# A graph network layer: the subtraction of h moved to TensorE, one normalised row of four moved to VectorE, three more edge groups read from the h table

## The reference

```
h    = relu(layernorm(x))
em   = relu(layernorm([h[src], h[dst]] @ msg_w + msg_b) * g + be) * edge_weight
msgs = segment_sum(em, dst) / count(dst)          # 0 where a node has no edge
gate = sigmoid(h @ gate_w + gate_b)
u    = relu(layernorm([h, msgs] @ upd_w + upd_b) * g_u + be_u)
out  = x + gate * u + (1 - gate) * h
```

## Time and profile before

| | us |
|---|---|
| median of 3 runs (1055.12 to 1071.27) | 1056.28 |
| profiled execution | 1053.59 |
| its span, first to last instruction | 1052.1 |
| busy in the span: PE / DVE / ACT / POOL | 729.7 / 833.7 / 811.5 / 605.7 |
| node stage, roughly | 0 to 560 |
| of it the steady loop, with clock 0.83 | 100 to 540 |
| edge stage, roughly | 560 to 1052 |

### The profile page before, as it was taken

How to read it: one execution, slowest core, us unless ns; L and a number is a source line. 1 busy time by engine, 2 the same in 40 slices (tenths; PEclk the granted TensorE clock), 3 DMA queues, 4 the chain that set the end, 5 groups by cost and what they waited for, 6 DMA issues and landing times.

```text
span 1052.1 us, 20637 instructions
## 1 busy us (share of the span) xinstructions
PE 729.7 (69%) x4448; PEld 588.4 (56%) x4448; DVE 833.7 (79%) x3740; ACT 811.5 (77%) x3396; POOL 605.7 (58%) x602
## 2 busy tenths in 40 slices
PE   2377686776767677777666547777777778778772
PEld 2256565654545556555545336666665667667661
DVE  7287888886877888778789347999999988888984
ACT  2378787877868788778779258999999977878973
POOL 5555555554545555555555746666666666665557
PEclk9787978887888887788776668999989888988986
DMA  5255655565655666566532211322221121111110
GB/s 147 76 177 175 209 182 190 187 200 179 196 173 192 215 198 199 171 200 206 192 117 68 90 38 62 95 92 83 94 89 54 62 70 54 61 63 58 65 67 34
DMA packets 74548, 133.66 MB, mean 127 GB/s; under 512 B 16134, under 2 KB 18006, under 8 KB 74482
## 3 DMA queue, kind: packets, MB, share of 16 engines
q1 hardware_dynamic: 53868, 97.58, 27.1%
q0 software_dynamic: 18912, 34.84, 11.8%
q10 hardware_dynamic: 1702, 0.53, 0.2%
HBM read 56.01 MB, written 80.81 MB: 130 GB/s over the span
## 4 chain that ended last, share of the span: by engine, by line
ACT 47%; PE 16%; another core or an unknown queue 15%; issue 11%; DVE 7%; POOL 3%; ACTq 1%; DMA 0%; DVEq 0%; POOLq 0%; SPq 0%
ACT hrow L406 14%; ACT junk L413 13%; ACT xload L406 4%; ACT work L444 3%; PE py L1290 3%; POOL out L626 3%; PE pt L1248 3%; ACT lnv L388 2%; PE pm L1313 2%; ACT work L1159 2%; PE pm L1315 2%; ACT rs L393 2%; ACT at L1099 1%; PE py L1254 1%
## 5 line engine op out<-in xcount | busy, mean ns | idle before, releaser
L626 POOL DMA_INDIRECT out<-work,sidx x196 | 202.7, 1034 | 135.3 <-issue 54.2
L413 ACT ACTIVATE junk<-py 128x128 bf16<-128x128 f32 x588 | 155.7, 292 | 74.8 <-remote 64.2
L621 POOL DMA_INDIRECT ring<-in_x,gidx x140 | 141.9, 1013 | 89.7 <-DVE work L465 47.4
L406 ACT ACTIVATE hrow<-xload,nb,rs 128x128 f32<-128x128 f32 x392 | 163.9, 525 | 1.6 <-issue 0.8
L621 POOL DMA_INDIRECT ring<-in_x,src_i x116 | 116.3, 1002 | 68.4 <-issue 31.5
L1290 PE MATMUL py<-w_u,work 128*128 128x129 f32 x784 | 144.9, 341 | 0.0
L1290 PEld LDWEIGHTS py<-w_u,work 128*128 128x128 f32 x784 | 122.7, 238 | 28.2 <-issue 28.2
L413 ACT ACTIVATION_READ_ACCUMULATOR junk<-py 128x1 f32 x588 | 130.7, 223 | 0.0
L1254 PE MATMUL py<-bias,ones 3*128 3x258 bf16 x294 | 66.8, 313 | 77.6 <-ACT work L1099 56.8
L621 POOL DMA_INDIRECT work<-in_x,gidx x56 | 55.8, 996 | 108.9 <-DVE work L465 97.9
L1248 PE MATMUL pm<-ident,work 128*128 128x128 f32 x376 | 72.4, 325 | 63.4 <-ACT work L1104 31.9
(11 more groups left out here) (179 smaller groups left out, 2049.0 us busy)
## 6 DMA issues: line engine op xcount, KB each, us to landing
xload<-in_x SPq DMA_DIRECT2D x98, 256.0 KB
normalised_rows<-hrow SPq DMA_DIRECT2D x98, 256.0 KB
out<-work SPq DMA_DIRECT2D x98, 256.0 KB
running_sums<-acc SPq DMA_DIRECT2D x49, 256.0 KB
staged_target_rows<-work SPq DMA_DIRECT2D x14, 256.0 KB
ring<-staged_target_rows SPq DMA_DIRECT2D x14, 256.0 KB, 2.8
out<-work,sidx POOLq DMA_INDIRECT x196
ring<-in_x,gidx POOLq DMA_INDIRECT x140
```

Of the source, the lines that this page charges most:

```text
L406: last = nc.scalar.activation(dest[:, m, :], rows[:, m, :], ACT.Relu, bias=nb[:, s4, at + m:at + m + 1], scale=rs[:, s4, at + m:at + m + 1])
L413: last = nc.scalar.activation(junk[:, j, k, :], prod[:, k, 0:H], ACT.Square, scale=scale, accum_out=mv[:, slot, at + k, 1:2])
L621: pool.indirect_dma_start(out=dest, out_offset=None, in_=rows, in_offset=bass.IndirectOffsetOnAxis(ap=idx, axis=0), **({} if rows is sums_ ...
L626: pool.indirect_dma_start(out=out, out_offset=bass.IndirectOffsetOnAxis(ap=idx, axis=0), in_=rows, in_offset=None, **if_tail).then_inc(s, 16)
```

## The change

- `turned(g)` groups (94 of 98): VectorE's four `mix` operations become one of 128x512, o = max(hrow, 0) + x. omg is no longer computed for them.
- TensorE's `back` becomes four transposes of the rectified rows and, into the same bank, four products of `ht_dst` (h transposed) with `minus_ident`, so that pm = u - h and L776 gives o = gt * (u - h) + (x + h), as before.
- One of the four h rows (LIFTED = 3) leaves ScalarE: VectorE makes it in `lifted_row`, as (x - mean) * rstd without the relu, right after `minus_mean`. So that row goes unrectified into `hrow`, into the h table and through the transposes; the relu is now in the moves out of PSUM (L1099, L1157: Copy becomes Relu) and in the max of the mix.
- New waits: SP's store of `hrow`, TensorE's `flip` wait for `lifted` as well; VectorE's `lifted_row` waits for the store of the group four before; ScalarE's move into `ht_dst` waits for `back` of the group four before, which now reads that buffer.
- One operation in the preparation makes `minus_ident`.
- LATE 29 becomes 26 and UPFRONT 10 becomes 13: edge groups 26 to 28 take their source rows from the h table, and 52 gathers instead of 40 stand between its completion and the first scatter.

```diff
 EARLY = 5
-LATE = 29
-UPFRONT = 10
+LATE = 26
+UPFRONT = 13
+LIFTED = G - 1
 REFILLED = 36
...
             "nb": 1,
-            "gain": 3,
+            "gain": 2,
+            "rest": 1,
             "mix": 1,
...
         }
-        nd = stages("node", {**common, "turned": 1, "back": 1})
+        nd = stages("node", {**common, "turned": 1, "back": 1, "lifted": 1})
         tl = stages("tail", common)
...
                              "gate": 2,
-                             "rest": 1,
                              "msgw": 1,
...
                 L.mark(nc.vector.reciprocal(gt[:, b, 0:n], e1[:, b, 0:n]))
-            else:
-                L.wait()
-                L.mark(nc.vector.tensor_scalar(omg[:, b, 0:n], gt[:, b, 0:n], -1.0, 1.0, ALU.mult, ALU.add))
+
+        def rest(dve, d, g, n=G):
+
+            d["gain"].after(dve, g)
+            b = g.at % 4
+            one_mark(d["rest"], dve, shifted(d, g), nc.vector.tensor_scalar(omg[:, b, 0:n], gt[:, b, 0:n], -1.0, 1.0, ALU.mult,
+                                                                            ALU.add))
...
                     nd["h"].after(sp, q)
+                    nd["lifted"].after(sp, q)
                     if q.turn is None and q.at == NG - 1:
...
                     row_stats(L, s, xload[:, s.at % XS, 1:2], 1)
-                if fin:
-                    gain(dve, nd, g, 2)
                 if new:
...
                     L.mark(row_stats(L, s, xload[:, s.at % XS, 2:4], 2))
+                if fin and not turned(g):
+                    rest(dve, nd, g)
                 if between is not None:
...
                     minus_mean(dve, nd, s.back(1), G)
+                if live(s.back(1), NG):
+                    lifted_row(s.back(1))
                 if new:
...
                     aggregate(L, s, G)
-                if fin:
-                    nd["gain"].after(dve, g)
+                if fin and turned(g):
+                    one_mark(nd["mix"], dve, g, nc.vector.scalar_tensor_tensor(
+                        o[:, g.at % 4], hrow[:, g.at % 4], 0.0, xload[:, g.at % XS], ALU.max, ALU.add))
+                elif fin:
+                    nc.vector.tensor_scalar(o[:, g.at % 4, LIFTED, :], hrow[:, g.at % 4, LIFTED, :], 0.0, None, ALU.max
+                                            ).then_inc(s_raised, 1)
+                    nd["rest"].after(dve, shifted(nd, g))
+                    dve.wait_ge(s_raised, g.at - TURNED + 1)
                     for k in range(G):
-                        last = mix_row(g, k, hrow[:, g.at % 4], xload[:, g.at % XS], o[:, g.at % 4])
+                        h = o if k == LIFTED else hrow
+                        last = mix_row(g, k, h[:, g.at % 4], xload[:, g.at % XS], o[:, g.at % 4])
                     one_mark(nd["mix"], dve, g, last)
-                    if not turned(g):
-                        beta(dve, nd, g, t_buf[:, g.at % 4], be_upd)
+                    beta(dve, nd, g, t_buf[:, g.at % 4], be_upd)
+
+            def lifted_row(g):
+
+                s4 = (g.at + 1) % 4
+                nd["rstd"].after(dve, g.back(-1))
+                if beyond(g, 4):
+                    dve.wait_ge(s_hst[g.at % 4], g.rounds(16))
+                one_mark(nd["lifted"], dve, g, nc.vector.tensor_scalar(
+                    hrow[:, g.at % 4, LIFTED, :], xload[:, g.at % XS, LIFTED, :], mv[:, s4, LIFTED, 0:1],
+                    rs[:, s4, LIFTED:LIFTED + 1], ALU.subtract, ALU.mult))
...
             assert prep_n[0] == BORDERS1, prep_n
+            dve.wait_ge(s_const, 2)
+            nc.vector.tensor_scalar(minus_ident[:, :], ident[:, :], -1.0, None, ALU.mult)
...
                 if live(g, NG):
-                    evacuate(nd, g, ht_dst[:, g.at % 4, :], pt[:, g.at % 2, :], ACT.Copy, "ht", "flip")
+                    node_ht(g)
                 node_h(s)
+
+            def node_ht(g):
+                if beyond(g, 4) and turned(g.back(4)):
+                    nd["back"].after(act, g.back(4))
+                evacuate(nd, g, ht_dst[:, g.at % 4, :], pt[:, g.at % 2, :], ACT.Relu, "ht", "flip")
...
                         act.wait_ge(s_hst[g.at % 4], g.rounds(16))
-                    one_mark(nd["h"], act, g, h_rows(g, hrow[:, g.at % 4], xload[:, g.at % XS], 0))
+                    one_mark(nd["h"], act, g, h_rows(g, hrow[:, g.at % 4], xload[:, g.at % XS, 0:LIFTED], 0))
...
                             act.wait_ge(s_staged[b], 16 * STAGED // 2)
-                    nc.scalar.activation(ht_src[:, g.at % 2, :], pt[:, 0, :], ACT.Copy)
+                    nc.scalar.activation(ht_src[:, g.at % 2, :], pt[:, 0, :], ACT.Relu)
                     ed["flip"].after(act, g)
...
                     if live(n, NG):
-                        evacuate(nd, n, ht_dst[:, n.at % 4, :], pt[:, n.at % 2, :], ACT.Copy, "ht", "flip")
+                        node_ht(n)
                     if turned(node.back(5)):
...
                         nd["final"].after(pe, g.back(1))
-                    one_mark(nd["back"], pe, g, flip(pm[:, :, :].rearrange("p k h -> p (k h)"), t_buf[:, g.at % 4]))
+                    for k in range(G):
+                        nc.tensor.matmul(pm[:, k, :], t_buf[:, g.at % 4, k, :], ident[:, :], start=k == 0, stop=False,
+                                         is_transpose=True)
+                    for k in range(G):
+                        last = nc.tensor.matmul(pm[:, k, :], ht_dst[:, g.at % 4, k * H:(k + 1) * H], minus_ident[:, :],
+                                                start=False, stop=k == G - 1)
+                    one_mark(nd["back"], pe, g, last)
                 g = s.back(4)
...
                     nd["h"].after(pe, g)
+                    nd["lifted"].after(pe, g)
                     one_mark(nd["flip"], pe, g, flip(pt[:, g.at % 2, :], hrow[:, g.at % 4]))
...
             def edge_step(s):
```

6 lines of the change are left out of this document (4 added, 2 removed).

## The result

The changed kernel takes 1090.56 us (median of 4 runs, 1084.9 to 1091.53) beside 1055.7 for the kernel before (1056.28 ahead of its fourth run): 1.0332 times its time, 95% interval 1.0279 to 1.0385. Forecast was 1022; the kernel is slower, as in the rival of 1100 us. The profiled execution of after took 1091.53 us, its span is 1090.4: 38.3 us more than before.

What follows compares the result with a forecast made beforehand. Node loop bound by VectorE and ScalarE at full clock (about 4.1 us), TensorE at half clock (5.1), plus TensorE stalls. Profiled 1053.6 - 34 (node loop) - 1 + 2 (edge stage) = 1020.6, forecast 1022 beside 1056.3; range 965 to 1105.

Steps and rivals of the forecast that it cites:

- the rival of 1100 us: Whole kernel slower, chance 0.28: stalls persist despite more PE work, half clock costs more; 5.75 us a step, 1100 us.
- the choice of the pattern of stalls: Node loop: stalls and half clock between the early and late edge stage's patterns, 4.9 us a step, -34 us.
- the sign I had given: Node loop, 100 to 540 us: if the forecast holds, clock 0.88 or more and unnamed share under 10%.
- My cycle sum: Node loop: a cycle's unstalled time divided by 4.1 us (full clock) and 7.0 (half) gives steps; 4.66, 5.2 or 6.45 each.
- its sign, a clock below 0.8: Node loop: clock below 0.8, with L1104 and L413 waiting for PE every step, would mean the slower case, chance 0.28.
- The good step: Node loop at full clock: PE becomes the bound at 3.7 to 4.58 us, taken as 4.1, no worse than 4.08.
- Half clock: Node loop at half clock: PE's extra products lengthen the step from 5.12 to 7.0 us, which nothing hides.
- Costs of nothing for the lifted row's waits: Node loop: VectorE's and ScalarE's waits for an earlier store of `hrow`, issued 2 to 3 steps ahead, cost nothing.
- The 12 gathers: Edge stage's start: 12 more gathers take 15.6 us, POOL idles 12.8, 2.8 show; +2 us, bounds 0 to 6.
- four steps later: Edge stage's start: the first scatter's successor needs it only four steps later, so the gathers' cost was put at +2 us.
- The sign that I had named: Near 640 us: a gap of POOL's scatters or VectorE waiting for `s_scat` would mean the gathers cost more than +2 us.
- this rival's price of nothing: Node loop: VectorE's lifted row could delay POOL's descriptor writing, at most 0.28 us a step, priced at nothing; no chance given.

Runs made afterwards that it cites:

- g2: Changed kernel without its four products with `minus_ident`, on an occasion with stalls: 1084.87 us, ratio 1.0166 to the kernel before.
- g1: Kernel before with only the changed kernel's TensorE products added, on an occasion with stalls: 1083.01 us, ratio 1.0175 to the kernel before.
- e2: Kernel before with only LATE 26 and UPFRONT 13 changed, on a quiet occasion: 871.78 us, ratio 1.0111 to the kernel before.
- e5: Changed kernel run again unaltered, on a quiet occasion: 846.28 us, ratio 0.9832 to the kernel before.
- e8: Changed kernel plus unread TensorE products ahead of `back`, 18, 8, 8 and 0 in four steps running: 1143.6 us, ratio 1.0710 to the kernel before.
- f1: Kernel before plus four unread TensorE products in every node step: 1067.69 us, ratio 1.0308 to the kernel before.

## Why the prediction was wrong

**The step that failed is the choice of the pattern of stalls**, "I choose between the first and second, 4.9". I read the low unnamed share of the edge stage as a property of PE's mix of work and took it over to the node loop. The clock did what I said (0.89, the sign I had given was 0.88 or more), but the unnamed share went to 21.7%, not below 10%, and the step to 5.55 us, not 4.9. Clock and stalls are separate things: a clock of 0.81 goes with 22.3% in g2, one of 0.89 with 15.7% in g1 and with 21.7% in after. The rule of the Trainium skill that the prediction cites (TensorE: Matmul & The Clock Gate, section HAM oscillation), which the trace bears out as far as the clock goes, would have misled in the same direction. My cycle sum comes near with the right sizes: the eight long pieces from 112.45 to 256.88 us are 20.6 us apart, 4.2 of it stalled, 22% (4.5 us) at half clock; 11.9 / 3.8 + 4.5 / 6.5 = 3.8 steps, 5.4 us each; measured 5.55. It should have been tried on the kernel before first: 7 / 4.1 + 6.8 / 5.12 = 3.0 steps in 17.3 us, 5.7 us each, where 5.28 was measured.

The slower rival was nearly right in its price, 1100 and 5.75 us a step with part of it absorbed, and in its premise that stalls have a cause which more PE work doesn't remove. The rest was partly luck. It kept the stalls as they were and put the whole loss on PE at half clock, while the runs show both more named time with the products (g1) and more stall time with the shorter work (g2); and its sign, a clock below 0.8, didn't come.

The last line of the sum is off by little: 1020.6 and 2.7 give 1023.3, not 1022.

**Full and half clock.** The good step was given 4.1 (3.7 to 4.58) and is 3.77 to 3.85: the sets of transposes queue up back to back, as in my lower bound. Half clock: 7.0 against 6.5. VectorE's new operation 0.67 and 0.66, the lifted row 0.28 and 0.35, so that VectorE's work is 3.99 a step with stalls (316.01 x 5.554 / 440), not 3.87. ScalarE 3.74 and 3.83. On a quiet occasion this part gives 80 x (4.06 - 3.77) = 23 us.

**Waits.** Costs of nothing for the lifted row's waits held: 1.5 us of idle time in 68 (L792 above).

**The 12 gathers** were given +2, bounds 0 to 6. The trace has 13 us between the first and the seventh store with stalls, and e2 has 10.1 us on the whole without. The error is the 12.8 us of POOL idle time that I netted against them: that time is waiting for h rows which themselves come later when the run of gathers is longer, so 10.2 us of it were still there after; and "four steps later" was no cover, since those steps pass in less time than the run takes. The sign that I had named, VectorE waiting for the scatter, is e5's L1014.

**The lifted row and POOL.** The prediction weighed, by the Trainium skill, SBUF, section Who interferes with whom, that VectorE could hold off POOL's descriptor writing. The gathers take 0.998 to 0.999 us each in the node loop of after and 0.996 to 0.997 before: no sign of it. So this rival's price of nothing stands. The bond that the rows do show runs between POOL's gathers and TensorE's results, and the prediction didn't weigh it.

**What stays open:** what the stalls are, and why one occasion has them and another doesn't. Of the 19 above 3 us in after, 18 end within some 2 us of a fall of the clock; they all but vanish where PE is saturated (e8, 1.7% of the chain); and they end behind unbroken runs of POOL's gathers. None of this is shown as the cause.

## What to carry to other kernels

Take the time of the kernel before on more than one occasion ahead of any working: here it is 861 or 1036 to 1072 us, and the same edit is 1.7% faster on the one and 3.3% slower on the other. Where the chain holds a large unnamed share, price an edit for both cases, with and without it, and don't let a saving on other engines count in full while that share is unexplained. Hold the end of each unnamed piece against the timelines of all engines, those off the path too, before you take its share as given. Idle time of an engine can only be netted against added work if what it waits for doesn't move with that work.

## What the runs showed of the hardware

- Without stalls the node loop of the kernel before runs at 4.06 us a group and a clock of 1.00 with 251 GB/s (e2); with them at 5.29, 0.83 and 192 GB/s. Chip 13 showed both (860 and 1072 us).
- A stall: TensorE's products are dispatched, VectorE or ScalarE waits up to 4.7 us for their results in the loop of after (5.84 once in before), and about its end the clock goes from full (2.4 GHz) to half (1.2 GHz) for 3 to 7 us. Of 150 such waits above 3 us in 14 profiles 147 end 0.5 to 1.6 us behind an unbroken run of POOL's gathers.
- At the edge stage's start an unnamed wait, its longest piece 12 to 33 us, lies beside POOL's run of indirect gathers, 14 us longer with 52 of them than with 40; on the quiet occasions the chain has no such piece beside the same run.
- More work for PE brings the clock from 0.83 up to 0.99, and the kernels with it are 1.8% (g1) to 7.1% (e8) slower than the kernel before. Products of 128x128 in float32 that nobody reads are no free filling: four a step cost 3.1% (f1), although PE's records fill only 318.59 of 440 us of the loop of before.
- No version that was run on both kinds of occasion is better on both. The changed kernel with 29 and 10 is the fastest on the quiet occasions (837.01 beside 861.67) and 1.9% behind with stalls; with 32 and 7 it equals the kernel before with stalls, and that one was not run on a quiet occasion.
